# Dense attention: weighing in three float32r passes, low parts on GpSimd, row sums by VectorE in PSUM

## The reference

```python
P, L, BATCH = 128, 4096, 2          # channels, tokens of an image, images
q, k, v = xn @ w_query, xn @ w_key, xn @ w_value
s = (q @ k.T) * P ** -0.5           # 4096 x 4096 for each image
out = x + softmax(s, axis=-1) @ v
```

## Time and profile before

| | us |
|---|---|
| median of 3 runs | 11067.49 (11067.43 to 11083.72) |
| the profiled execution, its own time | 11073.83 |
| its span | 11072.0 |
| this stage in it, first projection to last store's issue | 6479.55 to 7654.12 |
| TensorE busy over the span | 10046.5 (91%) |
| VectorE, ScalarE, GpSimd busy | 6934.8, 5276.4, 5609.9 |

### The profile page before, as it was taken

One profiled execution on the slowest core, in us unless ns is written; L12 is line 12 of the kernel. 1 busy time (PEld: TensorE's weight loads), 2 busy tenths in 40 slices (PEclk: granted clock), 3 DMA queues, 4 the chain that ended last, 5 costly groups with the idle time before them and its releaser, 6 DMA issues. The chain is left out here.

```text
span 11072.0 us, 146129 instructions
## 1 busy us (share of the span) xinstructions
PE 10046.5 (91%) x45360; PEld 7803.1 (70%) x45360; DVE 6934.8 (63%) x8005; ACT 5276.4 (48%) x13704; POOL 5609.9 (51%) x2968
## 2 busy tenths in 40 slices
PE   7999999999967699999999689998599999999977
PEld 5677677667743588888888456565388887888854
DVE  6677677667755699999999644343533333333337
ACT  4787787778743677777777222222111111111110
POOL 4797788779743699999999126463100000000000
PEclk9999999999987799999999789999799999999988
DMA  2111111111124544444444510001745555455521
GB/s 81 26 39 40 38 30 38 41 26 39 32 88 163 189 107 108 105 108 108 105 105 108 195 56 8 14 10 73 254 123 130 128 128 159 127 133 123 125 105 64
DMA packets 646817, 1018.65 MB, mean 92 GB/s; under 512 B 285816, under 2 KB 347776, under 8 KB 631552
## 3 DMA queue, kind: packets, MB, share of 16 engines
q1 hardware_dynamic: 646176, 1010.30, 32.8%
HBM read 717.21 MB, written 211.03 MB: 84 GB/s over the span
## 5 line engine op out<-in xcount | busy, mean ns | idle before, releaser
L687 POOL TENSOR_TENSOR l_probs_low<-l_probs,l_probs_high 128x512 fp32r<-128x512 f32 x1792 | 2385.8, 1361 | 795.3 <-ACT l_probs_high L657 781.6
L1374 POOL TENSOR_TENSOR m_c_h<-m_h,m_c 128x2048 f32<-128x2048 f32 x520 | 2341.9, 4578 | 45.9 <-DVE m_h L1361 45.7
L1361 DVE TENSOR_TENSOR_SCAN m_h<-m_decay,m_ps_x 128x1024 f32<-128x1024 f32 x1040 | 2272.4, 2262 | 92.3 <-issue 64.5
L1274 PE MATMUL m_ps_y<-m_c_h,m_ident 128*128 128x256 f32 x8320 | 1981.6, 381 | 2.2 <-POOL m_c_h L1374 2.2
L743 DVE TENSOR_REDUCE l_max_by_row<-l_ps_all 128x8 f32<-128x512 f32 x2048 | 1358.0, 685 | 524.9 <-PE l_ps_all L506 444.4
L1274 PEld LDWEIGHTS m_ps_y<-m_c_h,m_ident 128*128 128x128 f32 x8320 | 1512.8, 191 | 174.1 <-POOL m_c_h L1374 4.9
L655 ACT ACTIVATE l_probs<-l_ps_all 128x512 f32<-128x512 f32 x2048 | 1240.4, 606 | 452.8 <-PE l_ps_all L547 307.0
L2350 PE MATMUL s_ps_all<-s_toeplitz,s_u_high 128*128 128x512 f32 (+1 forms) x4608 | 1327.9, 372 | 59.4 <-DMA s_toeplitz<-filters 50.3
L657 ACT ACTIVATE l_probs_high<-l_ps_all 128x512 fp32r<-128x512 f32 x2048 | 1233.0, 602 | 0.0
L2404 ACT ACTIVATE s_filtered_high<-s_rows 128x512 fp32r<-128x512 f32 x384 | 242.8, 632 | 1764.3 <-DVE s_rows L2477 898.4
L2350 PEld LDWEIGHTS s_ps_all<-s_toeplitz,s_u_high 128*128 128x128 f32 x4608 | 845.9, 189 | 240.0 <-DMA s_toeplitz<-filters 51.3
(11 more groups left out here) (320 smaller groups left out, 15384.1 us busy)
## 6 DMA issues: line engine op xcount, KB each, us to landing
m_delta_u<-du_t SPq DMA_DIRECT2D x1040, 128.0 KB, 3.7
s_toeplitz_sums<-filters SPq DMA_DIRECT2D x192, 642.0 KB, 6.7
s_toeplitz_sums<-filters SPq DMA_DIRECT2D x192, 386.0 KB, 5.7
m_c<-c_windows SPq DMA_DIRECT2D x130, 512.0 KB, 4.2
s_toeplitz<-filters SPq DMA_DIRECT2D x64, 770.0 KB, 9.3
s_toeplitz<-filters SPq DMA_DIRECT2D x64, 642.0 KB, 10.4
l_q_and_row_bias<-l_q_parts SPq DMA_DIRECT2D x64, 512.0 KB, 5.0
du_t<-m_delta_u_high SPq DMA_DIRECT2D x128, 256.0 KB, 3.1
```

The costliest lines, as they stand in the source:

```text
L687: pool.tensor_tensor(pl[:, slot, :], pt[:, slot, :], f(ph[:, slot, :]), ALU.subtract).then_inc(low_pool, 1)
L1274: ins = pe.matmul(y_ps[:, group % 2, 0:DIRS * SPAN].rearrange("p (d t) -> p d t", d=DIRS), ident[:, :], ch[:, group % CH, :, n, :], start= ...
L1361: dve.tensor_tensor_scan(h[:, u % H, :], decay[:, pair % 2, ct, k % 2, :, :].rearrange("p n t -> p (n t)"), x_ps[:, u % X, :], 0.0, ALU.mu ...
L1374: pool.tensor_tensor(ch[:, group % CH, 2 * pair % DIRS:2 * pair % DIRS + 2, :, :].rearrange("p d n t -> p d (n t)"), h[:, 2 * pair % H:2 * ...
```

## The change

- v is split in a high and a low part, both float32r (`vh`, `vl`). ScalarE takes each tile's exponential twice, in float32 (`pt`) and in float32r (`ph`); GpSimd subtracts, `pl = pt - ph`. `weigh` adds vh·ph, vl·ph and vh·pl, four steps behind (`LAG` = 4).
- The sum of a row's tiles moves from GpSimd in SBUF to VectorE in PSUM bank 7 (`add_tile`; the last addition writes `total` in SBUF). `column_sums` makes four columns of it (one of each 128 queries), VectorE inverts 128 x 4 (`invert`), `spread_inverse` turns the inverses to 128 x 512 by four matmuls against the identity into bank 4, ScalarE copies them out (`take_inverse`), and `divide` follows at step 7.
- VectorE's queue is written step by step: maxima and additions are mixed. The units start at step 6 (`FIRST`), 8 in 5 steps; the turn is at step 28. The widening copy is gone: `turn` reads the maxima as a broadcast.
- An image is loaded in four chunks; the second image's load is issued once the first image's projections are done. Each projection job waits for the low part's writer (`taken`), for v too.

```diff
+    SLOTS, LAG = 8, 4
+    SUMS_AT, INVERSE_AT, FIRST, TURN_AT = 2, 4, 6, KT - 4
...
+            for row in range(BLOCKS):
+                b, j = row // NTB, row % NTB
+                if j == 0 and b + 1 < BATCH:
+                    sp.wait_ge(filled, (b + 1) * JOBS)
+                    load(b + 1)
...
-                    pe.wait_ge(wide_ok, row + 1)
+                    pe.wait_ge(max_ok, row + 1)
...
-                        pe.wait_ge(expd, row * KT + (i - 2))
+                        pe.wait_ge(rounded, row * KT + (i - 2))
...
+                def weigh(row, i, slot):
+                    pe.wait_ge(low_ok, row * KT + (i + 1))
...
+                def column_sums(row):
                     pe.wait_ge(added, row * KT + (KT + SLOTS))
...
+                def spread_inverse(row):
+                    pe.wait_ge(recip, row + 1)
...
+                        if i >= LAG:
+                            weigh(row, i - LAG, slot)
+                        elif not head:
+                            weigh(row - 1, KT + i - LAG, 1 - slot)
...
+                        act.wait_ge(scored, row * KT + (i + 1))
+                        act.wait_ge(weighed, row * KT + (i + 1))
+                        act.wait_ge(added, row * KT + (i + 1))
                         act.activation(pt[:, i % SLOTS, :], ps[:, i % 3, :], ACT.Exp).then_inc(expd, 1)
+                        act.activation(ph[:, i % SLOTS, :], ps[:, i % 3, :], ACT.Exp).then_inc(rounded, 1)
+                        if i == INVERSE_AT + 1 and j:
+                            take_inverse(row - 1)
...
+                    pool.wait_ge(rounded, row * KT + (i + 1))
+                    pool.wait_ge(weighed, row * KT + (i + 1))
+                    pool.tensor_tensor(pl[:, k, :], pt[:, k, :], f(ph[:, k, :]), ALU.subtract).then_inc(low_ok, 1)
...
+                def add_tile(row, i):
+                    dve.wait_ge(expd, row * KT + (i + 1))
+                    dve.wait_ge(added, row * KT + (i + SLOTS))
...
+                        if i == INVERSE_AT + 3 and j:
+                            divide(row - 1, j - 1)
...
+                            for u in range(units_before(i), units_before(i + 1)):
+                                take_max(row + 1, u)
...
+                        add_tile(row, i)
```

More of the change, by code:

```diff
@@ L1682, in _ @@
                 sp.dma_start(w[:, n, :], src).then_inc(const, 16)
+            sp.dma_start(raw_first[:, :], first_in).then_inc(const, 16)
             sp.dma_start(ident[:, :], ident_in).then_inc(const, 16)
[L1684 to L1693, removed]
+            load(0)
+            for row in range(BLOCKS):
[3 more added lines that the diff above has]
+                    load(b + 1)
+                tokens = slice(row * TW, (row + 1) * TW)
+                if row >= 2:
+                    sp.wait_ge(done, row - 1)
+                sp.dma_start(res[:, j % 2, :], x[:, tokens]).then_inc(res_in[j % 2], 16)
+                if row >= 1:
+                    before = slice((row - 1) * TW, row * TW)
+                    sp.wait_ge(done, row)
+                    sp.dma_start(x_out[:, before], o[:, (j + 1) % 2, :]).then_inc(stored[(j + 1) % 2], 16)
+            sp.wait_ge(done, BLOCKS)
+            sp.dma_start(x_out[:, (BLOCKS - 1) * TW:BLOCKS * TW], o[:, 1, :]).then_inc(stored[1], 16)
             for s in stored:
@@ L1726, in max_unit @@
                         pe.wait_ge(fetched, row + 1)
-                    if u >= 2 or not head:
+                    if u == 1:
+                        pe.wait_ge(inverted, row + 1 if head else row)
+                    if u >= 2:
                         pe.wait_ge(max_taken, row * UNITS + (u - 1))
@@ L1759, in attend @@
                 def attend(row, start, slot, head=False, tail=False):
                     queries, following = bass.ds(start, TW), bass.ds(start + TW, TW)
-                    unit = 0
                     for i in range(KT):
-                        if i == 2 and not head:
-                            finish(row - 1, 1 - slot)
+                        if i == SUMS_AT and not head:
+                            column_sums(row - 1)
+                        if i == INVERSE_AT and not head:
+                            spread_inverse(row - 1)
@@ L1767, in attend @@
                         if not tail:
[L1768 to L1771 removed]
+                            for u in range(units_before(i), units_before(i + 1)):
+                                max_unit(row + 1, u)
+                            if i == TURN_AT:
                                 turn(row + 1)
```

193 lines of the change are left out of this document (107 added, 86 removed).

## The result

The changed kernel's median is 11019.46 us (10995.09 to 11023.53, 5 runs) against 11067.49 of the kernel before (11065.08 to 11083.72, 5 runs): a ratio of 0.9945, 95% interval 0.9931 to 0.9958. In E1, with 6 and 22 runs, it is 0.9936 (0.9924 to 0.9948), 72 us by the medians. So it is faster, as forecast, by less than forecast: 48 to 72 us for 79.7.

A forecast was written before the change was run, and what follows sets the result against it. TensorE was taken to bound the attention rows. Terms -68.4 + 10 - 16.2 - 4 - 1.5 + 0.4 = -79.7 us took 11067.49 to 10988, own range 10968 to 11005, widened up to 11028.

The forecast's parts named there:

- the likeliest case: Whole program faster, TensorE still bounding the attention rows: 10988 us, own range 10968 to 11005, chance 0.80.
- the first rival: VectorE bounds the steps with units, its addition into PSUM costing 1.085 us: +26 us, 11014; chance 0.10.
- What bounds it: In the attention rows TensorE sets the pace, busy 397 of 400 us; a row is its work alone.
- Weighing: In each tile three float32r matmuls take 0.70 us for 0.86; 512 tiles, -81.6 us, clock taken as kept.
- Row sums: Per row, the spread of the inverses adds +14.2 us over 16 rows; column sums for the wide sum give -1.0.
- What must keep up: ScalarE, GpSimd and VectorE keep up with TensorE's plain tile of 1.63 us; VectorE is nearest, its addition at 0.69.
- The division among the units: Division at step 7 delays a maximum; TensorE waits at step 8, 0.8 us in 12 rows: +10, range 0 to 16.
- Between the images: Second image's load is covered by rows: TensorE's idle 14.07 us falls to 0.75, -13.3; clock kept, -2.9.
- The prediction's own sign: What would show the forecast right between the two images: under 2 us there.
- Start: At the stage's start q jobs run while later chunks land: -4 us, between 0 and -6.
- End: At the stage's end the chain up to the store's issue falls from 4.83 to 3.3 us: -1.5.
- The second rival: Tile additions and GpSimd exclude each other, 2.13 us a tile, row 69.3: 11110 us; chance 0.05.

The follow-up runs named there:

- E1: The changed kernel once more, unchanged, for a second trace and more times: 11008.49 us, ratio 0.9936 against the kernel before.
- E5: The changed kernel with the division moved from step 7 to step 27, behind all units: 11017.06 us, ratio 0.9944, stage 1101.38.
- E2: The changed kernel with VectorE's product written back to its PSUM bank, so the final addition has one SBUF input: 10993.62 us, ratio 0.9917, stage 1104.20.
- E3: The changed kernel with the weighing as one float32 matmul of 512 columns again, all else kept: 11082.8 us, ratio 1.0005, stage 1193.93.
- E6: The changed kernel with the wide sum and the 512-column reciprocal back, no spread and no copy of it: 10996.02 us, ratio 0.9931, stage 1103.87.
- E4: The kernel before with the new load alone (four chunks, second image's load ahead of its rows): 11054.86 us, ratio 0.9977, stage 1169.78.
- E7: The changed kernel with the loop over the images written out on TensorE, ScalarE and VectorE: 11010.04 us, ratio 0.9942, stage 1112.18.
- E8: The changed kernel with the running sum in SBUF, so all 480 additions have two SBUF inputs: 11016.1 us, ratio 0.9947, stage 1117.95.
- E9: The changed kernel with the edits of E2, E6 and E7 together: 10988.03 us, ratio 0.9922, stage 1087.01.
- E10: The kernel before once more, unchanged, for one more trace: 11073.86 us, stage 1185.82.

## Why the prediction came out as it did

The forecast was 10988 with a range of 10968 to 11028; the median is 11019, inside, and 11010.5 over all 11 runs. The mechanism of the likeliest case came: faster, with neither VectorE nor GpSimd a bound. The number is in part luck, for and against. The likeliest case's own range ended at 11005 (its named terms give only 10976 to 11001), and what reaches to 11028 was kept for the first rival, which did not come; the profiled execution's 10995.09 lies 1 us from the 10994.1 forecast for it, but 7.8 us of its distance come from the rest of the program. The sum is better judged by the stage, which gave 8.7 us less than forecast (70.96 for 79.7), point by point:

- **What bounds it** was right: the row is TensorE's work. The account gave 62.2 us for a row without stall; with the stall away the trace shows 62.14 (E5) to 62.36 (E2).
- **Weighing** was right: 0.235 a matmul, the tile 1.62, the clock 1.00 in the rows. E3 puts 80 us on it for 81.6, with slower steps that hide 6 us of TensorE's waits for the maxima (8.5 for 14.7).
- **Row sums**: E6 puts 0.92 a row on sums and spread, 12.9 us in the 14 distances, where I had 13.2 in all 16 (14.2 less 1.0), 0.83 each. Right as a term. What I had not weighed is that the exchange loses: it takes 3.36 us from VectorE, which has room, and gives 0.9 to TensorE, which has none.
- **What must keep up** was right, with the addition into PSUM at 0.691 as L1880 had it. The first rival (1.085 from L1883) didn't come.
- **The division among the units**: mechanism and place were right (step 8, once a row, 0.91 us), the size was not. The step that failed is the choice of L1883's median, 1.085, for the final addition, with 1.78 only as the range's end; it measured 1.647. The median was no price of the instruction but what its old place left of GpSimd's instruction, plus 0.55; at the new place it begins 0.19 behind a subtraction of 1.29, which leaves 1.10. By the prediction's own working a longer addition adds its length to the wait: 0.6 + 1.647 - 1.085 = 1.16, and E5 measured 1.17. The row came to 63.31 for 62.2 + 0.8: 0.3 in 12 rows, +3.7 us.
- **Between the images**: the load's cover was right, and the wait for the small reciprocal is 0.37 for the 0.75. The 2.62 us without releaser weren't in the sum: with the 0.37, +2.2 on the idle time. They stood in no row of before, since there the wait for the DMA hid them; E4 shows them, E7 takes them away. The prediction's own sign, under 2 us between the images, failed by them. With this pause the lower clock came back: 15.69 for 13.8, +1.9. The prediction named that loss as a condition ("If the clock is lost anyway, 2.9 are missing").
- **Start**: from the weight's DMA to the v jobs 23.3 us for 25.8, -2.5 where I took -4: +1.5. In E1's trace it is 21.8, the -4, but there the 32 passes between the images take 16.71: the two terms that hang on the clock vary by 1 to 1.5 us from trace to trace. **End**: from the sums to the store's issue 4.70 for 5.89, -1.2 for -1.5: +0.3.

These are 3.7 + 2.2 + 1.9 + 1.5 + 0.3 = 9.6 for the 8.7; the 0.9 over lies in terms that were not taken apart. The rest of the distance from 10988 to 11019, some 23 us, must then be outside the stage. No trace of an execution that long exists for the changed kernel, but rests of 9877 to 9913 us stand in the traces above, and medians of 5 runs carry them.

The second rival, the additions and GpSimd excluding each other, had its mechanism right for instructions with two SBUF inputs, and E8 is the kernel in which it should have come true. Its price was wrong: 69.3 us a row forecast, 63.29 measured in the mean. The turns it took for granted are there; the step that failed is what a pair of them takes, 2.13 with a crossing of 0.15 in every tile, where the traces show the turns to follow each other 0.12 to 0.14 closer than their lengths: about 1.85, which leaves the row to TensorE.

The Trainium skill, page "SBUF — State Buffer", section "Who interferes with whom", says that a VectorE instruction with two SBUF inputs and one of GpSimd that reads SBUF lock each other out of a shared port pair for the whole instruction. The traces agree: 1.647 us with two SBUF inputs, 0.691 with one (E2), beside the same subtraction, and in E8 no addition overlaps a subtraction by more than 0.14 us. Taken at its word it gave the 16 us end of the stall's range; the measured 12 x 1.17 = 14 is nearer to that than the 10 I chose.

## What to carry to other kernels

When an instruction with two SBUF inputs on VectorE is moved among others that another engine waits for, do not take the median of its old place: it lasts 0.55 us beyond whatever GpSimd instruction it meets, here 0.69 to 1.84, and the new place decides. If one of its inputs can be in PSUM, or it can stand behind the critical work, the question goes away. Weigh what an edit saves by the engine that saves it: 3.36 us of an engine with 30% free bought nothing, and the small matmuls of sums and spread on the bounding engine cost 0.9 a row. Where a long wait ends in the same place as a loop, removing it leaves the loop's own pause, so look for what the wait was hiding. Before gains of parts are summed, split each trace's stage into the same stretches: here the clock's differences in the heads looked like a gain of the combination.

## What the runs showed of the hardware

- VectorE writes a 128x512 float32 sum to PSUM from one PSUM and one SBUF input in 0.69 us, while GpSimd is busy 66% of the time (all 480 between 678 and 700 ns).
- VectorE's addition of two SBUF inputs and GpSimd's instructions with SBUF inputs took turns: the addition ended 0.55 us behind the GpSimd instruction it met, in the kernel before, the changed one, E3, E5 and E6. With all additions so (E8) they took 0.67 to 1.83 and GpSimd's up to 1.85, and the mean row stayed at 63.29 us for 63.31.
- The end of a loop's turn left TensorE without work for 2.6 to 3.1 us (the changed kernel, E1 to E5, E8) but for 0.93 in E6, and the same loop written out for none (E7, E9). Behind the pause the next 32 passes of projection ran at the 1.2 GHz level for a part, 15.69 us for 13.90.
- The rest of the program, outside the changed stage, differed by up to 37 us of 11000 between traces, and the four normalizing stages, 57 to 59 us or 66 to 72 each (with a granted clock of 0.83 or 0.50 in the 30 us shown in E10), went with most of it; a stage's own length repeated to about 1 us, and told effects of 2 to 10 us apart where the medians could not.
